# A four-layer graph network on one core: GpSimd waits for the landing of the preceding chunk only ahead of the third and the fifth chunk of a group

## What is computed

```python
# layer 0: an MLP on each edge, summed by destination
h   = relu(concat([x[dst], x[src], edge_attr]) @ W1 + b1)
out = segment_sum(h @ W2 + b2, dst)
# layer 1: features of the source, summed by destination, scaled by degrees
agg = segment_sum(features[src] * ci[src], dst) * cj
out = relu(where(in_deg > 0, agg, features) @ W.T + b)
# layer 2: summed the other way, by source (row = src, col = dst)
agg = segment_sum(norm * x[col], row);  out = relu(agg @ W.T + b)
# layer 3: gated messages of the destination, summed by source
gate = silu(edge_attr40 @ W1.T + b1) @ W2.T + b2 + adapt_logit
agg  = segment_sum(gate * h[dst] * cw * mj, src) / clip(segment_sum(mj, src))
# after each layer: x = layernorm(x + out)
```

## Time and profile before

| | |
|---|---|
| runs of the kernel before | 20211.77, 20238.29, 20250.66 us, median 20238.29 |
| the profiled execution | 20236.51 us |
| its span, first to last instruction | 20234.7 us |
| mean granted clock of TensorE | 0.661 |
| busy: TensorE, its weight loads, VectorE, ScalarE, GpSimd | 56%, 47%, 48%, 19%, 55% |

### The profile page before, as it was taken

The page is one execution under the profiler, slowest core; times in us unless marked ns, Lnnn a source line. Parts: engine busy times, 40 slices in busy tenths (PEclk is TensorE's granted clock), DMA queues, the critical chain, the costliest instruction groups (busy, mean ns, idle before and its releaser), DMA issues. The chain is left out here.

```text
span 20234.7 us, 302760 instructions
## 1 busy us (share of the span) xinstructions
PE 11419.2 (56%) x63600; PEld 9543.6 (47%) x63601; DVE 9780.5 (48%) x26342; ACT 3891.4 (19%) x10412; POOL 11133.6 (55%) x11410
## 2 busy tenths in 40 slices
PE   6666666666656666665666545554464334555545
PEld 5555555555534444343444444444453224444445
DVE  3555555555566666664111455555442225555556
ACT  1000000000122122222333111111122222333331
POOL 4555555555544454444555556666635666666663
PEclk9999999999966666665555555555555555555555
DMA  4333333333211111112333222222222222222222
GB/s 110 77 76 76 76 76 77 77 77 77 67 40 38 39 41 42 41 41 64 90 91 90 78 69 69 70 70 68 64 70 82 77 80 73 75 76 76 76 75 52
DMA packets 1574947, 1407.00 MB, mean 70 GB/s; under 512 B 982792, under 2 KB 1441691, under 8 KB 1570446
## 3 DMA queue, kind: packets, MB, share of 16 engines
q1 hardware_dynamic: 597320, 636.63, 12.3%
q0 software_dynamic: 410000, 462.80, 9.7%
q10 hardware_dynamic: 567508, 306.27, 5.6%
HBM read 984.46 MB, written 420.15 MB: 69 GB/s over the span
## 5 line engine op out<-in xcount | busy, mean ns | idle before, releaser
L1752 POOL DMA_INDIRECT order<-l_msg,l_uring x6250 | 6081.7, 973 | 4212.9 <-DMA order<-l_msg,l_uring 2071.4
L1895 PE MATMUL ps<-l_ordb,l_ohs 128*128 128x49 f32 x15040 | 3307.2, 414 | 2680.7 <-DVE acc L1795 1365.9
L1895 PEld LDWEIGHTS ps<-l_ordb,l_ohs 128*128 128x128 f32 x15040 | 3240.4, 332 | 2747.3 <-DVE acc L1795 1406.5
L548 POOL DMA_INDIRECT l_rows<-btab,l_sd x3125 | 3024.2, 968 | 2368.4 <-DMA l_rows<-btab,l_sd 1388.8
L1088 POOL DMA_INDIRECT l_rows<-y,l_sd x1875 | 1822.2, 972 | 1960.5 <-DMA l_sd<-in_sd 907.1
L1795 DVE TENSOR_TENSOR acc<-acc,ps 128x49 f32 x7520 | 1526.0, 206 | 2158.8 <-issue 1031.0
L689 PE MATMUL ps<-l_rhs,l_lhs 64*128 x6250 | 1455.8, 426 | 824.5 <-DVE l_rows L625 506.5
L689 PEld LDWEIGHTS ps<-l_rhs,l_lhs 64*128 64x128 f32 x6250 | 1358.7, 327 | 911.7 <-issue 910.2
L704 PE MATMUL ps<-l_ohe,l_hid 128*128 128x32 f32 x6250 | 1384.7, 402 | 606.4 <-ACT l_hid L734 606.4
L704 PEld LDWEIGHTS ps<-l_ohe,l_hid 128*128 128x128 f32 x6250 | 1351.8, 331 | 656.7 <-ACT l_hid L734 622.6
L1929 PE MATMUL ps<-l_win,l_oht 96*128 x6250 | 533.1, 241 | 1901.5 <-DVE l_oht L1817 876.6
(11 more groups left out here) (313 smaller groups left out, 14535.0 us busy)
## 6 DMA issues: line engine op xcount, KB each, us to landing
l_ordb<-order SPq DMA_DIRECT2D x752, 250.0 KB
l_dstb<-ids SPq DMA_DIRECT2D x250, 600.0 KB
order<-l_msg,l_uring POOLq DMA_INDIRECT x6250
order<-l_zero ACTq DMA_DIRECT2D x125, 775.0 KB
l_eat<-in_ea40P SPq DMA_DIRECT2D x625, 120.0 KB
gates<-l_made ACTq DMA_DIRECT2D x625, 120.0 KB
l_gin<-gates SPq DMA_DIRECT2D x125, 600.0 KB
l_rows<-btab,l_sd POOLq DMA_INDIRECT x3125
```

Of the source, the lines that this page charges most:

```text
L548: pool.indirect_dma_start(rows[:, t, :], None, d["btab"], bass.IndirectOffsetOnAxis(ap=sd[:, t, 0:1], axis=0)).then_inc(gat[c], 16)
L1752: pool.indirect_dma_start(d["order"], bass.IndirectOffsetOnAxis(ap=uring[:, t:t + 1], axis=0), msg[:, t, :], None).then_inc(sc[c], 16)
L1895: done = t.matmul(red[b % 2][:, k * MW:(k + 1) * MW], ohs[b][:, k, :], ordb[b][:, k, 0:MW], start=True, stop=True)
```

## The change

A tuple `SEAMS = (2, 4)` takes the place of the condition `if c:` in the three loops. GpSimd waits for the landing of the chunk ahead only ahead of the third (c = 2) and the fifth chunk (c = 4). Layer 1 has c = 0, 1, 2 alone and so keeps one of two such waits. The empty instruction (`nop`) behind each wait goes with it. Nothing is added or moved on another engine. The waits of the consumers for `gat[c]` and `sc[c]` stay, and so do GpSimd's waits for buffers.

```diff
+SEAMS = (2, 4)
...
                     pool.wait_ge(est[c], (g + 1) * 16)
                     pool.nop(nofuse=True)
-                    if c:
+                    if c in SEAMS:
                         pool.wait_ge(gat[c - 1], (g + 1) * 16 * CT)
                         pool.nop(nofuse=True)
...
                     if behind:
                         pool.wait_ge(gat[c], g * (16 * CT))
                         pool.nop(nofuse=True)
-                    if c:
+                    if c in SEAMS:
                         pool.wait_ge(gat[c - 1], (g + 1) * 16 * CT)
                         pool.nop(nofuse=True)
...
                     if gated:
                         pool.wait_ge(look_taken, g * NCH + c + 1)
                     pool.nop(nofuse=True)
-                    if c:
+                    if c in SEAMS:
                         pool.wait_ge(sc[c - 1], (g + 1) * 16 * CT)
                         pool.nop(nofuse=True)
```

## The result

The changed kernel takes 21115.4 us (median of 4 runs, 21039.7 to 21216.1) against 20244.5 us of the kernel before (4 runs, 20211.8 to 20257.5): a ratio of 1.0435, 95% interval 1.0411 to 1.0458. The forecast was 19180 us. The profiled execution took 21216.1 us, its span is 21214.0, 979.3 us longer than before. Lines of the changed file are one higher than before (L548 is now L549, L1752 is L1753).

The account below looks back on a forecast made before the run. GpSimd was taken as the bound in layer 0 and most of layers 2 and 3. Savings of 687 (layer 0), 0 (layer 1), 255 (layer 2), 85 and 30 us (layer 3) took 20236.5 to 19180 us; 8-in-10 range 18820 to 19620.

Follow-up runs that it names:

- e9: Kernel before, but in layers 2 and 3 all four landing waits a group replaced by a 64-column fill GpSimd waits for; 22323.2 us (ratio 1.1024).
- e6: Kernel before, but in layers 2 and 3 the waits ahead of chunks 2 and 4 replaced by a 1700-column fill GpSimd waits for; 20134.1 us (0.9978).

## What to carry to other kernels

A wait of a DMA-issuing engine for its own landing can be worth more than it costs: here it was a pause that the other engines needed, and in which most of TensorE's late counts came through. Before removing such a wait, look in the trace for signals that arrive in those pauses (a count recorded long after the matmul's end, a waiter that goes on only when GpSimd stands still), and price the change with those signals at the next pause that is left. Then put pauses where the issuing engine has slack, and take one away only where it has none, and read the semaphore's number behind a releaser's name before building on it.

## What the runs showed of the hardware

- TensorE's counts came up to 17 us (once 19.6 us) after their matmuls' rows had ended while GpSimd issued indirect DMAs 1.27 us apart, and mostly 1 to 2.5 us after the last of a run (92, 68 and 54 in 100 of the late ones in layer 0 and the long stretches of layers 2 and 3); VectorE's and ScalarE's within 0.02 us.
- Register instructions of VectorE and SyncE, 0.04 us at the median, took 0.7 us at times: 75 us of VectorE's time in layer 2 from the 41st group before, 500 us after, none with scatters 1.9 to 2.0 us apart.
- Pauses of 0.92 us between runs of five (e9) left a group as slow as none (50.1 and 50.8 us), pauses of 2.0 to 2.3 us brought it to 39.8 (e6); DMAs 1.9 to 2.0 us apart hold none up for over 1 us.
- Thirty empty instructions behind an indirect DMA on GpSimd cost nothing (gap 0.30 us); a 64-column fill that GpSimd waits for makes the gap 0.92 us, a 1700-column fill 2.28.
- One program ran at 20497 and at 20177 us in two sessions, steady to 0.5% within each, while the kernel before differed by 0.2% the other way (20243 and 20292).
